# Three-layer graph kernel: tile loops placed at block starts, a shorter GpSimd loop, and the message sums moved to TensorE

## What is computed

```python
ht  = einsum('nd,rdo->nro', h, W_rel[l])        # 16 tables, one for each relation
msg = ht[src, etype]
h_rel = segment_sum(msg, dst) + h @ W_loop[l] + b_rel[l]
z   = (h @ W_gat[l]).reshape(n, 4, 32)
e   = leaky_relu(el[src] + er[dst], 0.2)        # el, er: z against attn_l, attn_r
alpha = softmax of e over the edges of one dst
h_gat = segment_sum(alpha * z[src], dst) + b_gat[l]
hc  = concat(h_rel, h_gat) @ W_fuse + b_fuse    # layer 0: times sigmoid(hc @ W_gate ...)
h   = relu(hc)
```

## Time and profile before

| | |
|---|---|
| median of 3 runs | 4204.2 us (4196.84 to 4204.68) |
| profiled execution | 4196.3 us |
| its span | 4194.8 us, 18977 instructions |
| busy: TensorE products, weight loads | 713.2 us (17%), 354.9 us (8%) |
| busy: VectorE | 2589.9 us (62%) |
| busy: ScalarE | 458.4 us (11%) |
| busy: GpSimd | 2524.9 us (60%) |
| indirect DMAs of GpSimd's queue | 37.6% of 16 DMA engines, 452.73 MB |

### The profile page before, as it was taken

How to read it: one execution, slowest core, us unless ns; L and a number is a source line. 1 busy time by engine, 2 the same in 40 slices (tenths; PEclk the granted TensorE clock), 3 DMA queues, 4 the chain that set the end, 5 groups by cost and what they waited for, 6 DMA issues and landing times. The chain is left out here.

```text
span 4194.8 us, 18977 instructions
## 1 busy us (share of the span) xinstructions
PE 713.2 (17%) x1896; PEld 354.9 (8%) x1896; DVE 2589.9 (62%) x3225; ACT 458.4 (11%) x944; POOL 2524.9 (60%) x2681
## 2 busy tenths in 40 slices
PE   7630121121221220111111121220000000000000
PEld 5310000000100110000000000110000000000000
DVE  6325666666656564766666656564567776665666
ACT  4330111011111110111111111110000000000000
POOL 0257666555666646766666766646666655566563
PEclk9865555555555555555555555555555555555555
DMA  5765444433444444444444444444333333233232
GB/s 214 266 242 126 136 115 124 121 120 119 132 126 150 131 126 115 140 131 131 131 130 126 138 130 153 130 124 113 84 96 91 86 82 81 76 90 87 78 88 54
DMA packets 153682, 517.15 MB, mean 123 GB/s; under 512 B 47272, under 2 KB 54648, under 8 KB 140864
## 3 DMA queue, kind: packets, MB, share of 16 engines
q0 software_dynamic: 132384, 452.73, 37.6%
q1 hardware_dynamic: 21280, 64.25, 4.1%
HBM read 351.66 MB, written 165.18 MB: 123 GB/s over the span
## 5 line engine op out<-in xcount | busy, mean ns | idle before, releaser
L609 POOL DMA_INDIRECT meta_nat<-table,stage_head x1200 | 1137.4, 948 | 711.7 <-issue 563.0
L609 POOL DMA_INDIRECT late<-table,stage_mid x768 | 726.6, 946 | 234.0 <-issue 231.2
L609 POOL DMA_INDIRECT scratch<-table,stage_tail x558 | 527.5, 945 | 314.8 <-issue 314.5
L1042 PE MATMUL ps_mix<-ident,hr 128*128 128x128 f32 x75 | 35.7, 475 | 3167.2 <-DVE hg L1375 1662.6
L900 PE MATMUL ps_tab<-wrel,hT 128*128 128x512 f32 x600 | 402.3, 802 | 124.5 <-issue 106.2
L1352 DVE TENSOR_TENSOR meta_nat<-meta_nat,ps_cnt 128x2112 f32<-128x2112 f32 x75 | 176.3, 2350 | 366.4 <-issue 272.7
L1356 DVE TENSOR_REDUCE acc<-meta_nat 128x132 f32<-128x2112 f32 x75 | 290.3, 3871 | 7.7
L1042 PEld LDWEIGHTS ps_mix<-ident,hr 128*128 128x128 f32 x75 | 13.7, 182 | 3231.4 <-DVE hg L1375 1701.9
L1346 DVE TENSOR_REDUCE acc<-meta_nat 128x128 f32<-128x2048 f32 x75 | 281.9, 3759 | 0.0
L1315 DVE MEMSET scratch<- 128x1920 f32 x75 | 124.3, 1658 | 241.6 <-issue 241.6
L1356 DVE TENSOR_REDUCE acc<-scratch 128x132 f32<-128x2112 f32 x69 | 266.5, 3862 | 7.1
(11 more groups left out here) (189 smaller groups left out, 1516.4 us busy)
## 6 DMA issues: line engine op xcount, KB each, us to landing
table<-rows SPq DMA_DIRECT2D x50, 1040.0 KB
meta_nat<-table,stage_head POOLq DMA_INDIRECT x1200
late<-table,stage_mid POOLq DMA_INDIRECT x768
scratch<-table,stage_tail POOLq DMA_INDIRECT x558
meta<-meta_ranked POOLq DMA_DIRECT2D x1, 3250.0 KB
xin<-in_x SPq DMA_DIRECT2D x48, 64.0 KB, 4.4
table<-rows,stage_id POOLq DMA_INDIRECT x50
late<-in_dst SPq DMA_DIRECT2D x1, 402.8 KB
```

The costliest lines, as they stand in the source:

```text
L609: pool.indirect_dma_start(out=slots[b][:, k, :], out_offset=None, in_=table[l % 2], in_offset=bass.IndirectOffsetOnAxis(ap=index, axis=0)) ...
L1042: pe.transpose(mix[0], hr[:], ident[:])
```

## The change

The loops over tiles of GpSimd, ScalarE, TensorE and VectorE are placed so that their first instruction is loaded at slot 0 of a fetch block of 256 instruction slots. GpSimd's loop gets shorter, to 249 instructions: a tile's own index row holds 64 slots instead of 80, the third group of the middle goes to the block path, and the tail's tree becomes four Ifs in a row on the bits 8, 4, 2 and 1 of n. VectorE therefore stages the tail's indices in four copies, each at its own place. The tail of a tile of 64 slots and more is fetched as a whole group.

The messages are no longer reduced by VectorE. For each group TensorE accumulates 16 (tail: 15) products of the identity with a slot's 128 x 128 messages in PSUM bank `ps_rel`, over all groups of the tile. `s_part` is now counted by TensorE; GpSimd's `free` and `next_block` and VectorE's `end_tile` wait for it. VectorE reads the message sum from PSUM and carries only the 132 columns of z.

```diff
-ELL = BLOCK + PAIR
+ELL = BLOCK
+FIRST = BLOCK - PAIR
...
+        PIECES = (8, 4, 2, 1)
...
+        def tile_loop(eng, kind):
+
+            return nc.Fori(0, T, engines=[kind], head_slot={kind: 0})
...
             def free(b):
 
                 pool.wait_ge(s_acc, n_read[b])
+                pool.wait_ge(s_part, n_read[b])
                 pool.reg_add(n_group, n_group, 1)
                 pool.reg_add(n_read[b], n_group, 0)
...
-            def gather_tail(l, n, size, first=0):
-
-                with pool.If(bits(pool, n, size) > 0):
-                    for k in range(first, first + size):
-                        fetch(l, "T", 1 + k, stage_tail[:, k:k + 1])
-                    if size > 1:
-                        gather_tail(l, n, size // 2, first + size)
-                if size > 1:
-                    with pool.Else():
-                        gather_tail(l, n, size // 2, first)
+            def gather_tail(l, n):
+
+                first = 0
+                for size in PIECES:
+                    has = counter(pool, f"has_{nc.next_id()}", 0)
+                    pool.reg_alu(has, n, size, ALU.bitwise_and)
+                    with pool.If(pool.snap(has, min_val=0, max_val=size) > 0):
+                        for k in range(first, first + size):
+                            fetch(l, "T", 1 + k, stage_tail[:, k:k + 1])
+                    first += size
...
-                with pool.If(in_first > 3):
-                    free("M1")
-                    gather(l, "M1", stage_mid[:, 2 * PAIR:3 * PAIR])
...
-                with pool.Fori(0, T) as t:
+                with tile_loop(pool, POOL) as t:
                     tile(l, t)
...
+            def group(b, first=False):
+
+                pe.wait_ge(s_landed[b], n_land[b])
+                if b != "T":
+                    pe.reg_add(n_land[b], n_land[b], 16 * GROUPS[b])
+                if first:
+                    pe.wait_ge(s_h2, n_h)
+                K = GROUPS[b]
+                for k in range(K):
+                    mm = pe.matmul(ps_rel[:, 0:D], ident[:], slots[b][:, 1 + k, 0:D], start=first and k == 0,
+                                   stop=True, skip_group_check=True)
+                mm.then_inc(s_part, 1)
+
+            def tile(l, t):
+                n, pairs, in_first = load_slots(pe, t)
+                group("H", first=True)
+                with pe.If(in_first > 1):
+                    group("M1")
+                with pe.If(in_first > 2):
+                    group("M2")
...
+                    pe.wait_ge(s_tail, n_tail)
+                    group("T")
+                pe.reg_add(n_tail, n_tail, 1)
+                pe.reg_add(n_h, n_h, 1)
                 transpose_sums(l)
-                pe.reg_add(n_h, n_h, 1)
                 fuse(l)
                 gate(l)
                 half_table(l)
                 rest_of_table(l)
...
-            def stage_this_tail(t, in_first):
+            def stage_this_tail(t, n, in_first):
 
                 v.memset(messages("T", 1, PAIR), 0.0)
                 v.memset(logits_of("T", 1, PAIR), LEAST)
-                at = dve.snap(in_first * PAIR + t * ELL, min_val=0, max_val=(T + 1) * ELL - PAIR)
-                v.tensor_copy(stage_tail[:].bitcast(I32), ell_flat[:, bass.ds(at, PAIR - 1)]).then_inc(s_tail, 1)
+                first = 0
+                for size in PIECES:
+                    dve.reg_alu(piece_at, n, PAIR - 2 * size, ALU.bitwise_and)
+                    dve.reg_alu(piece_at, piece_at, dve.snap(in_first * PAIR + t * ELL), ALU.add)
+                    at = dve.snap(piece_at, min_val=0, max_val=(T + 1) * ELL - size)
+                    ins = v.tensor_copy(stage_tail[:, first:first + size].bitcast(I32), ell_flat[:, bass.ds(at, size)])
+                    first += size
+                ins.then_inc(s_tail, 1)
...
                 if not first:
-                    v.tensor_copy(slots[b][:, 0], acc[:]).then_inc(s_carried, 1)
+                    v.tensor_copy(slots[b][:, 0, D:ROW], acc[:, D:ROW]).then_inc(s_carried, 1)
...
-                v.tensor_reduce(acc[:, 0:D], messages(b, lo, K + 1).rearrange("p k d -> p d k"), AX.X, ALU.add
-                                ).then_inc(s_part, 1)
...
                 v.reciprocal(rden[:], acc_z[:, :, DH:EX]).then_inc(s_rden, 1)
-                v.tensor_tensor(hr[:], acc[:, 0:D], meta[:, bass.ds(t, 1), M_LOOP:M_X].rearrange("p o f -> p (o f)"),
+                dve.wait_ge(s_part, n_g)
+                v.tensor_tensor(hr[:], ps_rel[:, 0:D], meta[:, bass.ds(t, 1), M_LOOP:M_X].rearrange("p o f -> p (o f)"),
                                 ALU.add)
```

More of the change, by code:

```diff
@@ L8 @@
 AX = mybir.AxisListType
+POOL, ACTE, DVE, PEE = (mybir.EngineType.Pool, mybir.EngineType.Activation, mybir.EngineType.DVE,
+                        mybir.EngineType.PE)
 F32 = mybir.dt.float32
@@ L368, in hub_blocks @@
             now = counter(eng, f"now_{nc.next_id()}", 0)
-            eng.reg_sub(left, pairs, BLOCK // PAIR)
-            eng.reg_sub(blocks, pairs, 1)
+            eng.reg_add(left, n, PAIR - 1 - FIRST)
+            eng.reg_alu(left, left, PAIR.bit_length() - 1, ALU.logical_shift_right)
+            eng.reg_add(blocks, left, BLOCK // PAIR - 1)
             eng.reg_alu(blocks, blocks, (BLOCK // PAIR).bit_length() - 1, ALU.logical_shift_right)
@@ L717, in tile @@
                 pool.reg_add(n_tail, n_tail, 1)
-                with pool.If(pairs > BLOCK // PAIR):
-                    blocks, groups_of_block = hub_blocks(pool, pairs)
+                in_tail = tail_of(pool, n)
+                with pool.If(pairs > FIRST // PAIR):
+                    blocks, groups_of_block = hub_blocks(pool, n)
                     with pool.Fori(0, blocks) as b:
@@ L879, in _ @@
             for l in range(L):
-                with act.Fori(0, T) as t:
+                with tile_loop(act, ACTE) as t:
                     tile(l, t)
@@ L1070, in rest_of_table @@
                 pe.reg_add(n_e, n_e, 1)
-            n_h = counter(pe, "pe_h2", 2)
-            def tile(l):
+            n_h = counter(pe, "pe_h2", 1)
+            n_land = {b: counter(pe, f"pe_land_{b}", 16 * K if b != "T" else 0) for b, K in GROUPS.items()}
+            n_tail = counter(pe, "pe_tail", 1)
+            n_lowered = counter(pe, "pe_lowered", 1)
+            low = counter(pe, "pe_low", 0)
+            lower_by = counter(pe, "pe_lower_by", 0)
+            tail_lands = counter(pe, "pe_tail_lands", 0)
@@ new lines, in tile @@
+            def tile(l, t):
[5 more added lines that the diff above has]
+                    group("M2")
+                in_tail = tail_of(pe, n)
+                with pe.If(pairs > FIRST // PAIR):
+                    blocks, groups_of_block = hub_blocks(pe, n)
+                    pe.reg_mov(lower_by, 16 * PAIR)
+                    with pe.Fori(0, blocks):
+                        pe.wait_ge(s_lowered, n_lowered)
+                        pe.reg_add(n_lowered, n_lowered, 1)
+                        pe.reg_sub(low, n_land["M2"], lower_by)
+                        pe.reg_alu(n_land["M2"], low, 16 * PAIR, ALU.max)
+                        pe.reg_mov(lower_by, 16 * BLOCK)
+                        with pe.Fori(0, groups_of_block()):
+                            group("M2")
+                    pe.reg_mov(in_tail, 0)
+                with pe.If(pe.snap(in_tail, min_val=0, max_val=PAIR - 1) > 0):
+                    pe.reg_alu(tail_lands, n, PAIR - 1, ALU.bitwise_and)
+                    pe.reg_alu(tail_lands, tail_lands, 16, ALU.mult)
+                    pe.reg_add(n_land["T"], n_land["T"], tail_lands)
+                    pe.wait_ge(s_tail, n_tail)
+                    group("T")
+                pe.reg_add(n_tail, n_tail, 1)
+                pe.reg_add(n_h, n_h, 1)
@@ L1082, in _ @@
             for l in range(L):
-                with pe.Fori(0, T):
-                    tile(l)
+                with tile_loop(pe, PEE) as t:
+                    tile(l, t)
         @block.vector
@@ L1431, in tile @@
                     group("M2")
-                with dve.If(in_first > 3):
-                    group("M1")
-                with dve.If(pairs > BLOCK // PAIR):
-                    blocks, groups_of_block = hub_blocks(dve, pairs)
+                in_tail = tail_of(dve, n)
+                with dve.If(pairs > FIRST // PAIR):
+                    blocks, groups_of_block = hub_blocks(dve, n)
                     dve.reg_mov(lower_by, 16 * PAIR)
@@ L1444, in tile @@
                             group("M2")
+                    dve.reg_mov(in_tail, 0)
                 stage_next_mid(t)
-                in_tail = bits(dve, n, PAIR - 1)
-                with dve.If(in_tail > 0):
+                with dve.If(dve.snap(in_tail, min_val=0, max_val=PAIR - 1) > 0):
                     dve.reg_alu(tail_lands, n, PAIR - 1, ALU.bitwise_and)
@@ L1460, in _ @@
                     dve.wait_ge(s_rows, T + 1 + l * T)
-                with dve.Fori(0, T) as t:
+                with tile_loop(dve, DVE) as t:
```

50 lines of the change are left out of this document (28 added, 22 removed).

## The result

The changed kernel takes 4484.7 us (median of 4 runs) where the kernel before takes 4204.4 (4 runs): a ratio of 1.067, 95% interval 1.064 to 1.069. The forecast was 4118 us. The sign was wrong.

The account below looks back on a forecast made before the run. GpSimd's fetch slots were taken as the bound, with 656 us of further idle time to be had. Less 61, 10 and 30, plus 15, gave 4110 us, with 8 us for the median 4118; range 3700 to 4700.

Parts of the forecast that it names:

- What bounds the kernel: GpSimd's fetch slots of 1.25 us, 1084 us a layer; all that can be had is 656 us of its further idle time.
- (c): Steps between tiles, 7.2 us in layer 1: read as engines completing instructions slowly, 1.40 us each, while indirect DMAs stream.
- Sums on TensorE: 3,003 products at 0.45 us, 1,350 us busy, 7 us a group, covered by the next group's 20 us of fetching.
- the slow rate: Upper bound for a TensorE product: four instructions at 1.40 us each, 5.6 us.
- The slower rival: TensorE's completions become the bound; one 6.7 us GpSimd stop in each of 75 tiles, +500 us, 4620 us; chance 0.37.
- the other 36 take 50 us: Of the tail's 60 TensorE instructions some 24 go through quickly; the remaining 36 need 50 us.
- The argument against it: Layer 2's steps are quick again behind GpSimd's pause, so the completion limit may be an average that short pauses meet.
- layer 0's stores: GpSimd's store waits in layer 0, 90 us less 30 for the layer's end: half counted back, 30 us gained.
- 15 were counted and 70 were the bound: Layer 1: two more sequencer instructions a tile cost 0 to 70 us; 15 taken, nothing to be won.
- the forecast's 61: Layer 2's net gain: 131 us of tail waits less 20 staying, less 60 at first fetches, plus 10 at stores.
- Loop heads and the short loop: Loop heads on a block's first slot and GpSimd's 249-instruction loop: nothing gained.
- The fetch rival: Instruction block fetches caused the slow steps between tiles; these and late table counts go, 3647 us; chance 0.17.

Follow-up runs that it names:

- the first two traces: Kernel before and changed kernel, both unedited, on a chip whose number is not on record: 4204.4 and 4484.7 us.
- VectorE's sums: Changed kernel with message sums back on VectorE, its loops and index copies kept: 3787.8 us, ratio 1.0025 to the kernel before.
- the pause: Changed kernel with GpSimd clearing an unused buffer three times after the eighth fetch of layer 2's tiles: 3812.6 us, ratio 1.009 to the kernel before.
- unread products: Changed kernel with message sums on VectorE, plus TensorE products on constants that nothing reads or waits for: 3790.5 us, ratio 1.0035 to the kernel before.
- wide products with the moved normalization: Changed kernel with 4 products of 512 columns a group and layer 2's normalization behind the next tile's first group: 3662.4 us, 0.969 of the kernel before.

## Why the prediction was wrong

**What bounds the kernel** held: 867 instructions a layer, 1.25 us a slot, and only GpSimd's idle time moves. Two readings were off and changed nothing: the last output store lies behind the rows' third window, so 10 us and not 36 follow it, and the 0.42 us of a product is not in the earlier trace rows.

**Cause (c)** was read rightly as slow completion, as far as the traces go: TensorE's own rows now have 2.7 us for two instructions, within a straight row of products and with the loop heads placed. That it is a condition of some chips could not be seen in one trace. On chip 3 it is absent, and the kernel before is 426 us faster.

**The step that failed** is "Sums on TensorE": "I take 0.45 us in a row ... covered by the 20 us in which the next group is fetched". Issued alone the products are cheaper still (30 passes, 15 products, in 5.90 us of layer 2: 0.39 us). But what others wait for is the count behind 60 instructions, and that came 18 to 38 us later. Behind a burst the other bound that the text named applied, "the slow rate, 4 x 1.40 = 5.6 us a product": the slow passes of layer 0 make 5.4 us a product. I had used that rate to explain three waits of the kernel before and then did not charge it to 12,000 new instructions of the same engine.

**The slower rival** (0.37) named the mechanism: the tail's instructions land while the next tile's fetches stream, GpSimd wants the buffer, stops, and the stop lets TensorE catch up. For "the other 36 take 50 us" the tile of three groups has 38 us, ended by GpSimd's stop. Its price was wrong in kind: not 6.7 us in each of 75 tiles, but 17 to 22 us in seven tiles of three groups and nine of two in layer 2, 14 to 17 in four tiles of layer 0, and none over 7 in layer 1. It gave 4620 us; 4485 were measured. "VectorE's end of tile tens of us behind its last reduction" is the 16.07 and 30 us above.

**The argument against it**, that the limit "may be an average that a few short pauses meet", has a true half: the count does come once GpSimd pauses. It pauses only because it is stopped.

**The other terms.** At the level of the forecast, layer 0's stores gave back the 30 us foreseen. Layer 1 lost 69 us where 15 were counted and 70 were the bound, but only in part by GpSimd's steps: 35 us are waits for table rows, which the text had left at nothing there. On chip 3, where (c) is missing, layer 2 gains 68 us, and that this lies near the forecast's 61 is luck: the tails gave 39 of the 111 us expected (70 were to be had there, not 131), and the first fetches gained 23 where 60 were to be lost. Layer 0 gains 38 there, 30 of them at the tails, and layer 1 gains 6. VectorE is busy 1907 us (1,890). Loop heads and the short loop, "by my reading nothing": 3788 against 3779 us, 0.25% slower with the index copies, so nothing is gained at that level. The fetch rival's 3647 us lies near the 3665 of the other chips, but for another reason: there (c) is absent in the kernel before as well.

**Open.** Why chip 8 and that of the first two traces complete instructions slowly is not known; a core's own DMA traffic doesn't bring it about. Whether it stays with a chip was not seen. Every time on record comes with a granted clock, so from a recorded execution; whether the recording has a part in the slow steps was not tried. That TensorE's late count is the whole of the 281 us is argued, not shown: neither VectorE's sums nor the pause nor unread products were run at the slow level. No version was shown to beat both kernels at both levels: the wide products are 1 us off the kernel before at 4208 (one run) and 2.5% ahead of it at 3780; wide products with the moved normalization (0.969) were not run at 4208.

## What to carry to other kernels

When a trace shows one engine completing instructions at some slow rate, charge that rate to every instruction that the change adds to any engine, and look at who waits for the last one's count, not at when it was issued. Prefer few wide instructions for such work: 4 products of 512 columns cost 17 us more than 16 of 128 at the 3780 level (chips 7 and 3) and 277 less at the 4208 level (two chips, the wide ones run once). And take the kernel before along in every comparison on another chip, with its trace: the sign of a change can hang on the chip.

## What was unexpected

The same program on one core takes 3778 to 3790 us on six chips and 4208 on another, at the same fetch pace and nearly the same granted clock (0.57 and 0.56); 407 us of it are GpSimd's idle time. On the good chips TensorE carried 7,400 more product passes in layer 2 of one experiment, at 0.11 us each, and the count was seen as soon as the last of them had run. And products on constants in a row took 0.22 us each where the granted clock of that stretch was 1.00, against 0.39 us for the 15 tail products at 0.59 in the first trace: of the clock's two levels, 2.4 and 1.2 GHz, the first stretch was all at the upper, the second mostly at the lower.
